# The feed-forward residual and output of a gated cross-attention block, kept transposed

## The reference

```
x = x + tanh(g_xattn) * attention(layernorm(x), ctx)      # scores are sigmoid(q k / sqrt(32)), no softmax
n = layernorm(x)                                          # (x - mean) / sqrt(var + 1e-5), rows of 512
h = gelu(n[tokens of expert e] @ w1[e] + b1[e])           # 448 tokens, 512 -> 2048
x = x + tanh(g_ffn) * (h @ w2[e] + b2[e])                 # 2048 -> 512
```

## Time and profile before

| | |
|---|---|
| median of three runs | 1764.13 us (1761.93 to 1768.9) |
| the profiled execution | 1768.12 us, span 1766.5 us |
| granted TensorE clock, mean | 0.992 |
| TensorE busy | 1727.9 us |
| ACT busy | 774.2 us |
| DVE busy | 699.4 us |
| POOL busy | 214.3 us |

### The profile page before, as it was taken

How to read it: one execution, slowest core, us unless ns; L and a number is a source line. 1 busy time by engine, 2 the same in 40 slices (tenths; PEclk the granted TensorE clock), 3 DMA queues, 4 the chain that set the end, 5 groups by cost and what they waited for, 6 DMA issues and landing times.

```text
span 1766.5 us, 34823 instructions
## 1 busy us (share of the span) xinstructions
PE 1727.9 (98%) x12672; PEld 1526.4 (86%) x12672; DVE 699.4 (40%) x1320; ACT 774.2 (44%) x1004; POOL 214.3 (12%) x301
## 2 busy tenths in 40 slices
PE   6999999999999999999999998899999999999998
PEld 5888888888888888888888887799999999999997
DVE  4323323323323333333333323436455454536453
ACT  4545545445445455455455455333333333333331
POOL 1112212212112112112112111000000000000000
PEclk9999999999999999999999999899999999999999
DMA  7767767677577667577677677335343434435341
GB/s 234 199 180 210 203 193 211 186 202 215 159 203 222 172 198 222 173 203 212 179 205 218 174 203 218 124 113 174 123 165 117 154 122 157 140 113 170 130 161 33
DMA packets 186626, 308.70 MB, mean 175 GB/s; under 512 B 23728, under 2 KB 134576, under 8 KB 186512
## 3 DMA queue, kind: packets, MB, share of 16 engines
q1 hardware_dynamic: 160256, 222.05, 44.3%
q0 software_dynamic: 26256, 84.95, 14.0%
HBM read 221.07 MB, written 85.85 MB: 174 GB/s over the span
## 4 chain that ended last, share of the span: by engine, by line
PE 96%; DMA 1%; DVE 1%; issue 1%; ACT 0%; SPq 0%; DVEq 0%; POOLq 0%
PE fill_ps L475 40%; PE fill_ps L609 18%; PE scores_ps L627 18%; PE scores_ps L507 9%; PE heads_ps L521 9%; PE fill_ps L535 1%; PE fill_ps L573 1%; DMA k_scr<-k_stage 0%; PE heads_ps L643 0%; PE fill_ps L643 0%; PE scores_ps L475 0%; DMA probs<-WKT_in 0%; DMA k_st<-k_scr 0%; SPq L284 0%; DMA q_st<-q_scr 0%
## 5 line engine op out<-in xcount | busy, mean ns | idle before, releaser
L691 ACT ACTIVATE probs<-scores_ps 125x1792 f32<-125x1792 f32 x192 | 320.3, 1668 | 120.7 <-PE heads_ps L521 71.3
L609 PE MATMUL fill_ps<-wQ,wK 128*128 128x448 f32 x1536 | 331.7, 370 | 0.0
L475 PE MATMUL fill_ps<-ctx_hl,wK 128*128 128x250 f32 x2304 | 311.8, 285 | 10.8 <-DVE wK L838 8.6
L627 PE MATMUL scores_ps<-ctx_hl,wV 128*128 128x448 f32 x1536 | 318.7, 364 | 0.8 <-ACT x1nT L725 0.8
L475 PEld LDWEIGHTS fill_ps<-ctx_hl,wK 128*128 128x128 f32 x2304 | 285.4, 191 | 33.9 <-issue 30.4
L609 PEld LDWEIGHTS fill_ps<-wQ,wK 128*128 128x128 f32 x1536 | 288.4, 189 | 26.0 <-issue 0.4
L627 PEld LDWEIGHTS scores_ps<-ctx_hl,wV 128*128 128x128 f32 x1536 | 288.7, 188 | 20.9 <-issue 0.9
L475 PE MATMUL fill_ps<-wV,ctx_hl 128*125 128x512 f32 x1152 | 287.7, 399 | 2.2 <-DVE wV L838 2.2
L475 PEld LDWEIGHTS fill_ps<-wV,ctx_hl 128*125 128x125 f32 x1152 | 209.8, 187 | 51.8 <-issue 2.4
L434 POOL DMA_DIRECT2D k_scr<-k_stage x192 | 139.2, 725 | 795.4 <-DVE k_stage L887 746.1
L507 PE MATMUL scores_ps<-q_st,k_st 96*125 96x224 f32 x1536 | 203.2, 275 | 15.8 <-issue 5.4
(11 more groups left out here) (77 smaller groups left out, 1215.8 us busy)
## 6 DMA issues: line engine op xcount, KB each, us to landing
k_st<-k_scr SPq DMA_DIRECT2D x576, 125.0 KB, 3.0
v_sb<-w_in SPq DMA_DIRECT2D x96, 512.0 KB, 4.2
k_scr<-k_stage POOLq DMA_DIRECT2D x192, 250.0 KB, 3.8
ctx_raw<-ctxT_in SPq DMA_DIRECT2D x48, 500.0 KB, 5.4
q_st<-q_scr SPq DMA_DIRECT2D x192, 112.0 KB, 3.3
k_stage<-w_in SPq DMA_DIRECT2D x32, 512.0 KB, 3.6
q_scr<-q_stage POOLq DMA_DIRECT2D x64, 224.0 KB, 3.7
x_ln<-x_in SPq DMA_DIRECT2D x16, 448.0 KB, 4.4
```

The source lines that it names most:

```text
L475: last = pe.matmul(out_, lhsT(kt, a), rhs(kt, c), start=(kt == 0 and t == 0), stop=(kt == KT - 1 and t == 2))
L609: last = pe.matmul(hid_ps[k][:, 0:T], w1[:, slot, a, kt, k * P:(k + 1) * P], xt[:, d, kt, :], start=(kt == 0 and t == 0), stop=(kt == KT - ...
L627: last = pe.matmul(y_ps[:, dt, 0:T], w2[:, slot, a, k, dt * P:(dt + 1) * P], hid_hl[:, slot, d, k, :], start=(c == 0 and k == 0 and t == 0 ...
L691: nc.scalar.activation(probs[0:ST, s % 3], scores_ps[0:ST, :, 0:2 * L], ACT.Sigmoid, scale=SCALE).then_inc(s_probs, 1)
```

## The change

1. The residual is stored once, transposed and not normalised (`x1T`), beside it the mean and 1/sigma of each token (`stat`, 224 numbers of 4 bytes, two stores a batch). U turns x1 instead of x1n. The store of x1 goes, and so does the last part of `ln_x1`.
2. SP loads x1T as `xt_raw` and, with `load_norm`, mean and 1/sigma spread over the 128 partitions; DVE normalises there with four operations (`normalise`). For later experts both are loaded at chunk 3 and normalised at chunk 5 of the expert before.
3. The output stays transposed: `leave_y` makes gate times y plus the residual, to which `add_bias` has added gate times b2, and that is stored. `turn`, `add` and `last_turns` go. The output tensor is laid out transposed; the host's reshape turns it.
4. The first expert begins earlier: in body B - 1 hidden chunks 0 and 1 at steps 7, 8, 10 and 11, the first gelu at step 9, `xt_hi` and `xt_lo` at step 6, `normalise(0)` at step 5, `load_norm(0)` at SP's step 5 and w1 of chunk 2 at its step 6; in body B hidden chunk 2, one half ahead of O0 and one ahead of U0. w1 takes the place of wV and w2 that of wK. The last expert is peeled off the loop.

```diff
-    HIDDEN_AT = (9, 11)
+    HIDDEN_AT = {7: (0, 0), 8: (0, 1), 10: (1, 0), 11: (1, 1)}
...
+                    if known(b, B - 1) and s == 5:
+                        load_norm(0)
+                    if known(b, B - 1) and s == 6:
+                        load_w1(0, 2)
...
+            def load_norm(e):
+
+                if known(e, 0):
+                    alone(sp, full["Q"], KT * B)
+                    alone(sp, s_stat_st, 32 * NB)
+                if known(e, 1):
+                    alone(sp, s_stat_st, 32 * B)
+                alone(sp, s_normed, 2 * e)
+                for m in range(2):
+                    sp.dma_start(norm[:, m, :], scr["stat"][m][bass.ds(e * T, T)].partition_broadcast(P)
+                                 ).then_inc(s_norm_in, 16)
...
+                    if c == 3 and not known(e, E - 1):
+                        load_xt(e + 1)
+                        load_norm(e + 1)
...
-                    if (kind, i) == ("O", 1):
-                        alone(pool, s_x1, 2 * b)
-                        pool.dma_start(scr["x1"][bass.ds(b - 1, 1)].rearrange("a (t p) d -> p (a t) d", p=LT),
-                                       x1).then_inc(s_x1_st, 16)
...
+                        alone(pool, s_ln[1], LN_STEPS * b)
+                        for m, row in enumerate((mv[:, 1, :, 0], rstd[:, 1, :])):
+                            pool.dma_start(scr["stat"][m][bass.ds((b - 1) * L, L)].rearrange("(t p) -> p t", p=LT), row,
+                                           allow_slow_non_contiguous=True).then_inc(s_stat_st, 16)
...
-                        if known(b, B) and (kind, i) == ("U", 0):
-
-                            for k in range(2):
-                                hidden(0, 1, k)
+                        if known(b, B) and i == 0:
+                            hidden(0, 2, "OU".index(kind))
...
-            def turn(e, tt):
...
-            def last_turns():
...
                     if known(b, B) and s == 0:
-                        gelu(0, 0)
+                        gelu(0, 1)
+                        e_hi(0, 2, 1)
...
+            def normalise(e):
+
+                dve.wait_ge(s_xt_in, 16 * 2 * NB * (e + 1))
+                dve.wait_ge(s_norm_in, 32 * (e + 1))
+                bc = [norm[:, m, :].unsqueeze(1).broadcast_to([P, KT // 2, T]) for m in range(2)]
+                for half in range(2):
+                    nc.vector.tensor_tensor(xt_raw[half], xt_raw[half], bc[0], ALU.subtract).then_inc(s_centred, 1)
+                for half in range(2):
+                    dve.wait_ge(s_centred, 2 * e + half + 1)
+                    nc.vector.tensor_tensor(xt_raw[half], xt_raw[half], bc[1], ALU.mult).then_inc(s_normed, 1)
+
+            def add_bias(e):
+
+                dve.wait_ge(s_b2_in, 16 * (e + 1))
+                nc.vector.tensor_scalar(gb2[:], b2[:], gate[:, 1:2], None, ALU.mult).then_inc(s_gb2, 1)
+                dve.wait_ge(s_gb2, e + 1)
+                dve.wait_ge(s_res_in, 16 * NB * (e + 1))
+                for dt in range(KT):
+                    nc.vector.tensor_scalar(resT[:, dt, :], resT[:, dt, :], gb2[:, dt:dt + 1], None, ALU.add
+                                            ).then_inc(s_res, 1)
...
-                    nc.vector.tensor_scalar(yT[:, dt, :], y_ps[:, dt, 0:T], b2[:, dt:dt + 1], gate[:, 1:2],
-                                            ALU.add, ALU.mult).then_inc(s_yT, 1)
...
+                    nc.vector.scalar_tensor_tensor(out=outT[:, dt, :], in0=y_ps[:, dt, 0:T], scalar=gate[:, 1:2],
+                                                   in1=resT[:, dt, :], op0=ALU.mult, op1=ALU.add).then_inc(s_out, 1)
```

More of the change, by code:

```diff
@@ L51, in flamingo_block @@
     T = B * L // E
-    TT = T // 4
     NB = T // L
@@ L97, in bank_of @@
     def bank_of(b, kind, i):
+        if known(b, B - 1) and (kind, i) in BANK_BESIDE:
+            return BANK_BESIDE[kind, i]
         return (BANK_FIRST if known(b, -1) else BANK)[kind, i]
@@ L150, in experts @@
         body(1)
-        with eng.Fori(2, E) as e:
+        with eng.Fori(2, E - 1) as e:
             body(e)
+        body(E - 1)
     with ExitStack() as ctx:
@@ L174, in flamingo_block @@
         x_ln = sb("x_ln", [P, 2, D])
[L175 to L177 removed]
+        x_pair = sb("x_pair", [P, 2, 2, D])
+        x_res, x1 = x_pair[0:LT, 0], x_pair[0:LT, 1]
         xnT = sb("xnT", [P, 2, KT, L], F32R)
         oT = sb("oT", [P, 2, KT, L], F32R)
[L180 removed]
+        x1T = sb("x1T", [P, KT, L])
         ident = sb("ident", [P, P])
@@ L405, in _ @@
             experts(sp, expert)
[L407 to L412, removed]
+            for dt in range(KT):
+                sp.wait_ge(s_out, KT * (E - 1) + dt + 1)
+                sp.dma_start(out[E - 1, :, dt, :], outT[:, dt, :]).then_inc(s_last_stored, 16)
+            sp.wait_ge(s_last_stored, 16 * KT)
         @block.gpsimd
@@ L814, in expert @@
                     e_hi(e, 1, 0)
-                for c in range(C):
-                    if c + 1 < C and not (first and c == 0):
+                for c in range(2 if first else 0, C):
+                    if c + 1 < C:
                         e_hi(e, 1, c + 1)
-                    if not (first and c == 0):
-                        e_hi(e, 2, c)
-                        gelu(e, c)
+                    e_hi(e, 2, c)
+                    gelu(e, c)
             ctx_hi(0, 0, 0, 0)
@@ L988, in expert @@
                     leave_y(e - 1)
-                for c in range(C):
-                    if c + 1 < C and not (first and c == 0):
+                for c in range(2 if first else 0, C):
+                    if c + 1 < C:
                         e_lo(e, 1, c + 1)
-                    if not (first and c == 0):
-                        e_lo(e, 2, c)
-                    for tt in ([0], [1, 2], [3])[c] if c < 3 and not first else []:
-                        add(e - 1, tt)
-                    if not (first and c == 0):
-                        split_hidden(e, c)
+                    e_lo(e, 2, c)
+                    split_hidden(e, c)
+                    if c == 5 and not known(e, E - 1):
+                        normalise(e + 1)
+                    if c == 6:
+                        add_bias(e)
             ctx_lo(0, 0, 0)
@@ L1004, in _ @@
             leave_y(E - 1)
-            dve.wait_ge(s_res_in, 16 * E)
-            for half in range(2):
-                dve.wait_ge(s_last_turned, (half + 1) * KT // 2)
-                cols = slice(half * D // 2, (half + 1) * D // 2)
-                for pair in range(2):
-                    rows = res[:, 2 * pair:2 * pair + 2, cols]
-                    nc.vector.tensor_tensor(rows, last_turn_ps[half][pair][0:TT], rows, ALU.add).then_inc(s_last_out, 1)
 def build(nc, io, out):
@@ L1019, in build @@
         "q": nc.dram_tensor("q_scr", (2, 2, 128, L), F32).ap(),
-        "x1": nc.dram_tensor("x1_scr", (B, L, D), F32).ap(),
-        "x1nT": nc.dram_tensor("x1nT_scr", (B, D, L), F32).ap(),
+        "x1T": nc.dram_tensor("x1T_scr", (B, 128, D // 128, L), F32).ap(),
+        "stat": [nc.dram_tensor(f"{name}_scr", (B * L,), F32).ap() for name in ("mean", "rstd")],
     }
```

164 lines of the change are left out of this document (78 added, 86 removed).

## The result

The changed kernel takes 1891.53 us (median of 4, 1884.2 to 1894.08) against 1764.32 (median of 4, 1761.93 to 1768.9): 1.0714 times the time before, 95% interval 1.0697 to 1.0732. The prediction was 1753.6, range 1743 to 1761. To judge small differences between single runs: executions of the kernel before, taken beside the experiments, lie between 1760.39 and 1768.98.

What follows compares the result with a forecast made beforehand. TensorE, busy for 98% of the span, was taken to bound the kernel. Gains of 12 (transposes) and 3.5 (tail) less 5 (handover) made 10.5 us, taken from the median 1764.1: 1753.6, range 1743 to 1761.

Steps and rivals of the forecast that it cites:

- The term of the attention stage: Attention batches: the new statistics stores delay K7's store by two or three covered microseconds; nothing on TensorE, 0 us.
- The four-byte stores are slow: Rival: late statistics stores hold SP in expert 0 before w1 of chunk 4, wait 18 us, total 1771.6; chance 0.06.
- Transposes: Expert stage: removing four transpose groups per boundary saves 1.7 us at each of seven boundaries; gain 12, bounds 11 and 13.
- Tail: After the last y matmul: one operation from PSUM and a 224 KB store end the span earlier; gain 3.5, bounds 3 and 4.
- DVE's work in the expert loop: Expert loop: normalise (4.4 us) and add_bias (3.2 at most) fit into existing cover and gaps on DVE; cost nothing.
- Handover: Last batch to first expert: K7 waits for normalisation, TensorE loses 6.6 us, clock 6; sum +5, bounds -3 and +11.
- Table loads: Handover, ACT: two further switches around gelu, taken at 1.28 us each; the skill's 2.66 would hold ACT 2.8 longer.

Runs made afterwards that it cites:

- run 5: Changed kernel with the means still stored as 224 four-byte pieces, but 1/sigma's store replaced by two pieces of 448 bytes (timing only): 1827.12 us.
- run 1: Kernel before, with only the two stores of 224 four-byte pieces per batch added on POOL ahead of K7's store: 1895.15 us, beside 1764.82 before.
- run 2: Changed kernel with each statistics store made of two 448-byte pieces from the identity matrix, same number, bytes and waits (timing only): 1750.08 us.
- run 7: Changed kernel with 2 x 224 pieces of 256 bytes instead of four; the experts read identity rows stored in two-piece stores (timing only): 1758.32 us.
- run 9: Changed kernel with the four-byte pieces written 64 bytes apart; the experts read identity rows stored in two-piece stores (timing only): 1757.83 us.
- run 12: Run 11 with SP's step 2 reordered, K2's gather ahead of expert_start: 1746.79 us (median, n = 7), 0.9895 times before.
- run 6: Changed kernel with the 2 x 224 four-byte pieces written 512 bytes apart; the experts read identity rows stored in two-piece stores (timing only): 1753.26 us.
- run 10: Changed kernel with the four-byte pieces written 16 bytes apart; the experts read identity rows stored in two-piece stores (timing only): 1757.61 us.
- run 3: Changed kernel with the same four-byte stores issued behind K10's store (K7's in the last batch) instead of behind U: 1850.6 us (n = 4), 1.0473 times before.
- run 4: Changed kernel with the true statistics turned into rows by two small transposes and stored once as four 448-byte pieces: 1756.78 us (n = 4), 0.995 times before.
- run 8: Changed kernel with the same four-byte stores issued by SP at its step 7 instead of by POOL: 1894.13 us.
- run 11: Run 4 with the norm loads of expert 0 moved from SP's step 5 to its step 2: 1750.87 us (n = 6), 0.9914 times before.

## Why the prediction was wrong

**What failed.** The term of the attention stage: "ahead of K7's store ... two or three microseconds of delay are covered. Nothing on TensorE: 0". Two things in it were wrong. The price of the stores was taken at two or three microseconds, near the b2 load's 2.8; in their place are 16.15 us for the pair, and 7.1 for one (run 5). And the delay was followed on POOL's queue alone. While the stores are on their way the DMA engines count as busy, transfers of SP's queue land late too, and the first to suffer is the context load of step 7, which has a cover of one step, not four. It costs 8.6 us a batch in the mean, 121 up to the last; run 1 brings this loss into the kernel before, run 2 takes it out of the changed one. The question that would have found it is not "who stands behind this store in its queue" but "which transfer of any queue has the least cover in the next 16 us".

**The rival that was nearly it.** *The four-byte stores are slow* had the mechanism, and its 12.1 us per store (24 for the pair) bounds the measured 16.15 from above. It charged them once, in expert 0, at 18 us, and got 1771.6; TensorE's wait there was 11.85. For the attention batches, where 121 us are, the prediction names +1 us a batch under this rival, and the 1771.6 does not even hold these. Its chance, 0.06, was low for a form of store that no row showed. The Trainium skill (DMA: Bandwidth & Descriptors, section Specifications) has transfers under 512 bytes done as read-modify-write; the pieces of 448 bytes (3.0 us), 256 bytes (3.2) and the lone four-byte ones (3.0 to 3.4) are under that limit and cheap here, so the rule alone doesn't tell the expensive case from the cheap ones.

**The other terms**, by run 2, in which only the pieces differ. Their directions held, their sizes less well:

- *Transposes*: 12 forecast (bounds 11 and 13), 15.1 measured: 79.5 to 77.37 a period. Two things are in it. Without transposes and with the groups at the lengths of the earlier trace rows a period is 78.08, as forecast and as in runs 7, 9 and 12; against the mean of before, 79.53, that is 1.45 a period, 10.1 in all. The prediction took 1.69 from the first period, the longest of the seven. The other 5.0 are hidden groups at 4.86 us where before had 4.96, which no term foresaw.
- *Tail*: 3.5 forecast, 4.9 measured. The span ends at 1890.2 with the last bias operation at 1887.16 of 0.68, 2.4 us before; the landing of the 224 KB store is 1.9, where 3.3 to 3.7 was taken from the earlier trace rows:

```profile
out<-probs SPq DMA_DIRECT2D x4, 224.0 KB, 1.9
```

- *DVE's work in the expert loop*: nothing, as forecast; the period shrank by more than the transposes.
- *Handover*: +5 forecast, +4.4 measured. The mechanism came as worked out: K7 waits for DVE behind the norm loads, and hidden(1,0), scores 11 and hidden(2,0) wait 1.08, 0.84 and 2.50 (forecast 1.5, 1.1, 2.5). That the size came out too is luck, two errors that cancel. Counted from the first mark, since run 2 comes to it 2.6 us earlier, the norm loads went out when forecast (17.5 us behind it), but the second took 6.55 to land where the Q row's 3.3 was taken, and K7 started at +29.4 where +25.6 was forecast: 3.8 later, behind an idle TensorE of 11.04 us where 6.6 was forecast. From K7 to the end of y of chunk 0 it then took 44.7 us, only 1.6 over the 43.1 at full clock, where 6 (bounds 3 and 9) had been put for the clock. The mean granted clock, 0.91 against 0.90 before, hides this: more than half of what it lacks to 1.00 falls into the wait for the norm loads, in which TensorE has nothing to do.
- *Table loads*: the two further switches cost 1.28 us each, with the activation right behind, as ScalarE's timeline of run 2 shows:

```profile
1114.10 1.28 ACT L799 ACT_TABLE_LOAD   x1
1115.40 1.16 ACT L799 ACTIVATE x_ln<-fill_ps,b_sb 128x448 f32<-128x448 f32 x2
1116.57 1.28 ACT L678 ACT_TABLE_LOAD   x1
1117.87 1.66 ACT L678 ACTIVATE probs<-scores_ps 125x1792 f32<-125x1792 f32 x1
```

Each activation starts 1.30 us after its load does, and between the end of gelu (1116.56) and the next load there is nothing. The 2.66 us a switch of the Trainium skill (ScalarE: Activation LUTs, section What ACT_TABLE_LOAD costs) isn't borne out by this trace.

The sum was 1753.6, and run 2, without the expensive pieces, measured 1750.08. This is closer than the terms are: by the spans of the profiles, which the terms were read from, the gain is 18.2 where 10.5 was forecast, and the forecast was then taken off a median 4 us below the profiled execution. The stores' term was 0 and should have been about +141.

**What stays open.** Why four-byte pieces next to each other are expensive: runs 6, 9 and 10 place it by distance, none shows the mechanism. What TensorE waited for in run 3. And why the expert period is 77.37 in the changed kernel and in runs 2 to 6, 8, 10 and 11, but 78.08 in run 7, run 9 and the profiled execution of run 12 (hidden groups of 4.96 instead of 4.86): 5 us over seven periods, enough for the 4.6 us that run 9 stands above run 6.

## What to carry to other kernels

Price a store by the form in which it meets memory, not by its bytes: 896 bytes in 224 touching four-byte pieces took 7.1 us to land and made transfers of the other queue late, at 77 us for the kernel; both stores, turned into rows first, landed in 3.6 us, and the turning cost the kernel 6.7. Where a trace has no row for a form of transfer, it belongs among the terms with a bound per execution of its loop, and is to be set against the transfer with the least cover on any queue. A change that does several things is worth taking apart after a bad result: of this one, everything but the form of two small stores was together a gain of 14 us (run 2), and the handover within it a loss.

## What the runs showed of the hardware

- Two stores of 224 four-byte pieces at adjacent addresses take 16.15 us to land (one takes 7.1), and the DMA engines show a busy share of 1.07 at 25 GB/s in such a stretch. 16 bytes apart they land in 4.1 and 5.1, 64 bytes apart in 3.2 and 3.4, 512 bytes apart in 3.0 and 3.2, and the same count of 256-byte pieces in 3.2.
- It is the same from SP's queue (1894.13) and from POOL's (1891.53).
- With such stores behind K10's (run 3) TensorE stops with no releaser in the profile: for 6.0 to 12.5 us where the loop over pairs of batches jumps back (1.4 at most before), and for up to 2.6 us inside a group of matmuls.
- A kernel's period of matmuls can come out at 77.37 or 78.08 us with the same work in it (runs 6 and 9).
